# Routed experts on TensorE: one table load per four pairs, down product two pairs behind, inner transposes in two banks

## What is computed

```python
x = x + gated_scan(layernorm(x))                      # (16, 512, 256)
h = layernorm(x)
top-2 of 16 experts by softmax(h @ router_w)
routed = sum over the two: prob * (silu(h @ g_e) * (h @ u_e)) @ d_e
out = x + routed + (silu(h @ sg) * (h @ su)) @ sd      # 8192 tokens, D = 256, F = 128
```

## Time and profile before

| what | before |
|---|---|
| runs | 772.11, 772.59, 775.65 us |
| span of the profiled execution | 772.7 us, 0.1 us above the median of the runs |
| first stage | to about 430 us |
| expert stage, row transposes of pair 0 to the last down product | 430 to 692 us |
| last send of a result, then gathering and output | 697 us, to 772.7 us |
| TensorE busy, share of the span | 78% |
| granted TensorE clock in the expert stage from 440 us | 1.00 |

### The profile page before, as it was taken

How to read it: one execution, slowest core, us unless ns; L and a number is a source line. 1 busy time by engine, 2 the same in 40 slices (tenths; PEclk the granted TensorE clock), 3 DMA queues, 4 the chain that set the end, 5 groups by cost and what they waited for, 6 DMA issues and landing times.

```text
span 772.7 us, 16380 instructions
## 1 busy us (share of the span) xinstructions
PE 601.8 (78%) x3710; PEld 499.9 (65%) x3741; DVE 539.9 (70%) x1660; ACT 321.6 (42%) x733; POOL 368.3 (48%) x516
## 2 busy tenths in 40 slices
PE   3689899999999999999974788988988988970000
PEld 2467777777778777778763677877877877750000
DVE  8778898888899988897866245545445444545776
ACT  4366455565555565555452233333333333330000
POOL 3214445654545644445647356556556656661000
PEclk9789999999999999999997699999999999995555
DMA  4994111110101111101114434434544444417998
GB/s 155 275 330 125 38 40 50 56 48 34 48 34 56 55 41 41 48 34 57 57 45 171 117 120 156 155 114 155 156 131 148 146 135 146 147 50 247 379 385 293
DMA packets 82806, 96.91 MB, mean 125 GB/s; under 512 B 10142, under 2 KB 74066, under 8 KB 82774
## 3 DMA queue, kind: packets, MB, share of 16 engines
q1 hardware_dynamic: 61270, 54.32, 23.3%
q0 software_dynamic: 13056, 33.84, 12.1%
q10 hardware_dynamic: 8448, 8.39, 3.1%
HBM read 52.04 MB, written 46.57 MB: 128 GB/s over the span
## 4 chain that ended last, share of the span: by engine, by line
PE 57%; issue 12%; DVE 9%; DMA 7%; ACT 3%; POOL 2%; SPq 1%; DVEq 1%; POOLq 0%; ACTq 0%
PE gd L600 14%; PE tr L398 8%; PE gu L405 5%; DMA raw_w<-expert_results 5%; PE tr L405 5%; PE gd L436 5%; PE dn L405 5%; PE gu L617 4%; PE dn L617 4%; PE cb L398 3%; PE misc L405 2%; PE misc L527 2%; DVE tokens L1293 1%; SPq L383 1%; DMA expert_rows<-row_buf,slot 1%
## 5 line engine op out<-in xcount | busy, mean ns | idle before, releaser
L1355 POOL DMA_INDIRECT expert_rows<-row_buf,slot x128 | 132.0, 1031 | 145.3 <-DVE slot L1011 107.2
L1423 POOL DMA_INDIRECT expert_results<-raw_w,row_ids x144 | 141.6, 983 | 67.9 <-issue 35.2
L600 PE MATMUL gd<-w_hi,bx 128*128 x576 | 112.0, 297 | 0.6 <-DVE bx L1235 0.6
L436 PE MATMUL gd<-wgd,xT 128*128 128x512 f32 x384 | 103.0, 405 | 4.6 <-DVE xT L936 4.6
L398 PE MATMUL tr<-ident,row_buf 128*128 128x128 f32 x416 | 64.6, 279 | 46.4 <-issue 32.9
L1235 DVE TENSOR_TENSOR bx<-tr,bx 128x512 fp32r<-128x512 f32 x72 | 49.8, 692 | 71.6 <-ACT bx L820 63.7
L398 PEld LDWEIGHTS tr<-ident,row_buf 128*128 128x128 f32 x416 | 49.1, 142 | 64.1 <-issue 57.8
L600 PEld LDWEIGHTS gd<-w_hi,bx 128*128 128x128 f32 x576 | 85.1, 192 | 3.1 <-issue 1.0
L820 ACT ACTIVATE bx<-tr 128x512 fp32r<-128x512 f32 x71 | 42.5, 599 | 101.2 <-PE tr L398 101.2
L436 PEld LDWEIGHTS gd<-wgd,xT 128*128 128x128 f32 x384 | 71.7, 196 | 18.9 <-DVE xT L936 3.1
L1254 DVE TENSOR_TENSOR raw_w<-gd,raw_w 128x256 f32<-128x256 f32 x72 | 30.6, 425 | 64.7 <-ACT raw_w L826 64.7
(11 more groups left out here) (155 smaller groups left out, 1250.0 us busy)
## 6 DMA issues: line engine op xcount, KB each, us to landing
row_buf<-expert_rows SPq DMA_DIRECT2D x144, 130.0 KB, 2.1
raw_w<-expert_results SPq DMA_DIRECT2D x32, 512.0 KB, 10.9
tokens<-in_x SPq DMA_DIRECT2D x16, 512.0 KB, 4.9
out<-tokens ACTq DMA_DIRECT2D x16, 512.0 KB, 7.1
expert_results<-raw_w,row_ids POOLq DMA_INDIRECT x144, 2.4
expert_rows<-fill_rows SPq DMA_DIRECT2D x17, 130.0 KB, 2.6
raw_w<-in_gate_w SPq DMA_DIRECT2D x16, 128.0 KB, 4.3
raw_w<-in_up_w SPq DMA_DIRECT2D x16, 128.0 KB, 4.4
```

The source lines that it names most:

```text
L436: pe.matmul(gd[j % 2][:], xT[a][:, c, j * P:(j + 1) * P], wgd[b][:, c, :], start=(a, b, c) == (0, 0, 0), stop=False)
L600: last = pe.matmul(bgu[p][:, h * 2 * F:(h + 1) * 2 * F], bx[a][:, p, (h * KC + c) * P:(h * KC + c + 1) * P], gate_up_w[b][:, bass.ds(at[h] ...
L1355: pool.indirect_dma_start(out=rows, out_offset=bass.IndirectOffsetOnAxis(ap=slot[:, q, choice, j:j + 1], axis=0), in_=row_buf[:, q, j, :], ...
L1423: pool.indirect_dma_start(out=results, out_offset=bass.IndirectOffsetOnAxis(ap=row_ids[:, at, h:h + 1], axis=0), in_=y[:, w, h, :], in_off ...
```

## The change

TensorE's order is written as `four_pairs`. One load stands at its head, of 12 registers from word 252 + 8i on (eight from word 256 on for i = 0), and serves the tiles of pairs 4i - 2 to 4i + 3. The slot of pair q is now: row transposes of pair q + 1, inner transposes of pair q - 1, gate and up of pair q, down product of pair q - 2. The down product comes one slot later than before, and so does `results_out` on DVE. The inner transposes alternate between the banks `cb` and `misc`, and wait for ACT's copy of the pair before the last one instead of the last. The loop has the same 16 turns; behind it stand one more `four_pairs` and the last two down products, which need no load of their own. There are 18 loads in place of 37. SP and POOL are unchanged.

```diff
--- before.py
+++ after.py
@@ -578,11 +578,12 @@
 
             gate_up_w = [w[:].rearrange("q e w -> q (e w)") for w in (w_hi, w_lo)]
             down_w_flat = w_down[:].rearrange("q e d -> q (e d)")
-            btr, bgu, bth, bdn = (tr[0], tr[1]), (gd[0], gd[1]), cb, (gu, dn)
-            regs = [pe.alloc_register(f"weight_reg{k}") for k in range(6)]
-
-            def rows_transposed(q, w, p, n):
-
+            btr, bgu, bth, bdn = (tr[0], tr[1]), (gd[0], gd[1]), (cb, misc), (gu, dn)
+            regs = [pe.alloc_register(f"weight_reg{k}") for k in range(12)]
+
+            def rows_transposed(q, m, n):
+
+                p, w = m % 2, m % 4
                 pe.wait_ge(rows_in[w], 2 * W * (n + 1))
                 if known(q, 2):
                     pe.wait_ge(bx_lo, q - 1)
@@ -605,9 +606,9 @@
 
             def inner_turned(q, p):
                 pe.wait_ge(binner, q + 1)
-                if known(q, 1):
-                    pe.wait_ge(bh_ready, q)
-                transposes(bth, 0, [b_inner[:, p, h * F:(h + 1) * F] for h in range(2)], bth_done)
+                if known(q, 2):
+                    pe.wait_ge(bh_ready, q - 1)
+                transposes(bth[p], 0, [b_inner[:, p, h * F:(h + 1) * F] for h in range(2)], bth_done)
 
             def down(q, p, at):
                 pe.wait_ge(bh_ready, q + 1)
@@ -623,40 +624,35 @@
                 pe.load(use, table[0:1, bass.ds(first, count)])
                 return [pe.snap(r, min_val=0, max_val=(E - 1) * D) for r in use]
 
+            def four_pairs(i, last=False):
+
+
+                behind = 4 if known(i, 1) else 0
+                at = weight_at(8 * i + 2 * P - behind, 8 + behind)
+                for m in range(4):
+                    q = 4 * i + m
+                    here = behind + 2 * m
+                    if not (last and m == 3):
+                        rows_transposed(q + 1, (m + 1) % 4, i + (m == 3))
+                    if known(q, 1):
+                        inner_turned(q - 1, (m + 1) % 2)
+                    if isinstance(q, int) and q == 0:
+                        pe.wait_ge(w_lo_ready, E // 2)
+                        pe.wait_ge(w_down_in, W * E)
+                    gate_up(q, m % 2, at[here:here + 2])
+                    if known(q, 2):
+                        down(q - 2, m % 2, at[here - 4:here - 2])
+                return at
+
             pe.wait_ge(tab_ready, 1)
-            rows_transposed(0, 0, 0, 0)
-            at = weight_at(2 * P, 4)
-            rows_transposed(1, 1, 1, 0)
-            pe.wait_ge(w_lo_ready, E // 2)
-            pe.wait_ge(w_down_in, W * E)
-            gate_up(0, 0, at[0:2])
-            rows_transposed(2, 2, 0, 0)
-            inner_turned(0, 0)
-            gate_up(1, 1, at[2:4])
-            down(0, 0, at[0:2])
-
-            def two_pairs(q, w, n, last=False):
-
-                at = weight_at(2 * q + 2 * P - 2, 6)
-                rows_transposed(q + 1, w + 1, 1, n)
-                inner_turned(q - 1, 1)
-                gate_up(q, 0, at[2:4])
-                down(q - 1, 1, at[0:2])
-                if not last:
-                    rows_transposed(q + 2, (w + 2) % 4, 0, n + (w == 2))
-                inner_turned(q, 0)
-                gate_up(q + 1, 1, at[4:6])
-                down(q, 0, at[2:4])
-
-            two_pairs(2, 2, 0)
+            rows_transposed(0, 0, 0)
+            four_pairs(0)
             with pe.Fori(1, PAIRS // 4 - 1) as i:
-                two_pairs(4 * i, 0, i)
-                two_pairs(4 * i + 2, 2, i)
-            two_pairs(PAIRS - 4, 0, PAIRS // 4 - 1)
-            two_pairs(PAIRS - 2, 2, PAIRS // 4 - 1, last=True)
-            at = weight_at(2 * P + TILES - 2, 2)
+                four_pairs(i)
+            at = four_pairs(PAIRS // 4 - 1, last=True)
             inner_turned(PAIRS - 1, 1)
-            down(PAIRS - 1, 1, at)
+            down(PAIRS - 2, 0, at[8:10])
+            down(PAIRS - 1, 1, at[10:12])
 
 
         @block.scalar
@@ -809,7 +805,7 @@
                 act.wait_ge(bth_done, q + 1)
                 if known(q, 2):
                     act.wait_ge(bdn_done, q - 1)
-                act.activation(b_innerT[:, p, :], cb[:, 0:2 * F], ACT.Copy).then_inc(bh_ready, 1)
+                act.activation(b_innerT[:, p, :], (cb, misc)[p][:, 0:2 * F], ACT.Copy).then_inc(bh_ready, 1)
 
             def pair(q, p, last=False):
 
@@ -1253,20 +1249,19 @@
                     dve.wait_ge(bth_done, q - 1)
                 dve.tensor_tensor(b_inner[:, p, :].rearrange("q (h f) -> q h f", h=2), gu_bank(p)[:, :, F:2 * F],
                                   b_silu[:, p, :].rearrange("q (h f) -> q h f", h=2), ALU.mult).then_inc(binner, 1)
-                if known(q, 1):
-                    results_out(q - 1, (w + 3) % 4, n if w else n - 1)
+                if known(q, 2):
+                    results_out(q - 2, (w + 2) % 4, n if w >= 2 else n - 1)
 
             dve.wait_ge(bx_hi, 1)
             rows_rest(0)
-            pair(0, 0, 0)
-            pair(1, 1, 0)
-            for q in range(2, 8):
+            for q in range(8):
                 pair(q, q % 4, q // 4)
             with dve.Fori(2, PAIRS // 4 - 1) as i:
                 for w in range(4):
                     pair(4 * i + w, w, i)
             for q in range(PAIRS - 4, PAIRS):
                 pair(q, q % 4, q // 4, last=q == PAIRS - 1)
+            results_out(PAIRS - 2, 2, PAIRS // 4 - 1)
             results_out(PAIRS - 1, 3, PAIRS // 4 - 1)
```

## The result

The changed kernel takes 746.09 us as the median of four runs (743.62 to 748.6), the kernel before 772.35 us as the median of its four. The ratio is 0.964 with a 95% interval of 0.961 to 0.968: 26.3 us less. The forecast was 761.0 us, within 742 to 765. The time lies in the range, but the gain is more than twice the 11.6 us that I had worked out, so the sum was wrong.

The account below looks back on a forecast made before the run. TensorE was taken to bound the expert stage, idle behind table loads; 11.8 us over 16 turns plus 0.5 behind the loop, less 0.7 at the end, made 11.6 us less: 761.0 us, range 742 to 765.

Parts of the forecast that it names:

- What bounds the stage: Expert loop: TensorE bounds it, 86% busy, its idle time all ahead of row transposes, where table loads hold up the sequencer.
- The load that goes: Mid-turn load of slot 4i + 2 disappears: slot 25 takes 3.12 us instead of 4.00, slot 26 takes 3.02 instead of 2.97.
- the price of the load that stays: Load of 12 registers behind the loop's branch: three pieces of 16 bytes, about 1.60 us, bounds 0.67 and 3.07; chance 0.40.
- The tail: End of the stage: result copies one slot later make the last sends slip by 0.7 us, bounds 0 and 3.
- pair 71's load: Behind the loop: the load ahead of pair 71's transposes goes, with its 0.50 us of idle time.
- A: Rival on the 12-register load: an aligned load is one read whatever its length, 0.67 us, total 745.2 us; chance 0.23.
- C: Rival on the 12-register load: 246 ns per register, 3.07 us, slower than before at 786.0 us; chance 0.17.
- B2: Rival on the 12-register load: two reads, widest piece at each step, 1.12 us, total 752.8 us; chance 0.12.
- D: Rival on the loop's slots: load time goes but slots don't shorten, DVE's product or POOL too late, 770.7 us; chance 0.08.

Follow-up runs that it names:

- the grid: The kernel before with 96 table loads in 24 forms added on TensorE behind its last down product, each load's last register used in a small product; 822.92 us.
- e4_down_one_behind: The changed kernel with down product and result copies one pair behind as before, load still 12 registers from word 252 + 8i; 745.52 us, ratio 0.966 to the kernel before.
- e3_once_unaligned: The changed kernel with the down product one pair behind again and its one load per turn ten registers from word 254 + 8i; 787.91 us, 1.022 of the kernel before.

## Why the prediction was right, and where it was wrong

**What bounds the stage** was right: TensorE, with its idle time behind table loads and nowhere else. No wait for a semaphore came in its place, POOL still fits into a turn, and the granted clock stayed at 1.00.

**The load that goes** was right. The slot that had held it took 3.10 us (forecast 3.12), the next one 2.95 (3.02).

**The step that failed is the price of the load that stays.** I put the 12 registers at 1.60 us, and they take 0.85. The reading behind it was "one read costs 475 ns and the instruction 50", with pieces as wide as start and length allow. It met all the rows, 525 to 534 ns and 1476 ns, and was false in every part. By the grid the six registers from word 258 are not three reads but six steps, and the two registers at 688.2 (532 ns) are two steps, not one. The four from word 256 (525 ns) are one step of 332 ns in the grid; in the program they were TensorE's first load, and the changed kernel's first load too is dearer: eight registers take 781 ns there (the minimum of its row) and 592 to 612 elsewhere, some 0.19 us more in both cases. So I had read a price of two steps, and one of one step and a first load, as the same price of a read. That the number of pieces for 12 registers, three, came out right is luck: the same reading gives three pieces of 8 bytes for six registers from word 256, where the grid shows a step of four registers and two of one. A step of 16 bytes costs some 0.26 us and not 0.48. The difference of 0.75 us, 17 times, is 12.8 us of the 14.7 by which the gain was missed.

**The rest of the miss** in the loop is 0.08 us in the slot with the load and small amounts in slots 24 to 26, together 12.90 - 12.76 = 0.14 us a turn beyond the load (12.90 is the forecast turn with the load at its measured price), 2.2 us.

**The tail** was named and sized too small: 0.7 us forecast, 15.09 - 13.76 = 1.3 measured, within the bounds of 0 and 3, and e4_down_one_behind shows that it comes from the later down product.

**Sum of the terms as measured**: 26.1 us for the turns, 0.7 for pair 71's load (its slot takes 2.95 us in place of 3.61; 0.5 forecast), less 1.3: 25.5, against 26.3 between the medians.

**The rivals.** A gave 745.2 us, next to the result, but for 0.67 us and "whatever its length", which is false: 8, 12 and 16 registers take 0.59, 0.85 and 1.11. The argument that I held against A was false too: SP's eight registers from word 0 do start at a multiple of 16 bytes and span 32, and took 534 ns. C was right about the loads of before (one price per register, 246 ns) and wrong in extending it to the new one; e3_once_unaligned is what C describes, a load over the 2.28 us at which the prediction put the loss: 2.66 us, and 1.022 of the time before. B2, two reads, gave a load of 1.12 us and fell with it. Of D nothing came: the slots kept their length.

The Trainium skill gives 200 ns per register for loads from HBM (Runtime: NRT & Kernel Launch, Instruction fetch mechanics). The unaligned loads from SBUF here come near it, at 240 to 270 ns per register; those from a start at 16 bytes, at 69 to 77 ns per register for 8 to 16 registers, don't. The Trainium skill's floor of about 600 ns for such a load (DMA: Bandwidth & Descriptors, Latency and other measured facts) is not borne out here: one register took 306 ns, four took 332.

**What was the gain, then?** The alignment. The two factors, crossed: unaligned twice 14.39 us a turn, unaligned once 14.4 to 16.0, aligned twice 12.42, aligned once 12.76. Halving the loads made the turn longer: the load behind the branch, the dearest place, then has three steps in place of two, and the aligned load in mid-turn that goes had cost nothing (its slot takes 3.11 us with it and 3.10 without). The later down product cost 1.3 us at the end, and the second bank gave 0.8 us at most.

## What to carry to other kernels

TensorE's load of registers from SBUF was paid here in steps of some 250 ns; start such a load at a multiple of 16 bytes and take a multiple of four registers, even if some are not used, and count the steps rather than the loads. Place it behind queued work and not next to a branch: here 0.59 us disappeared in mid-turn, and 0.85 us cost 0.15 there and 0.69 behind the branch. A model that meets four rows without remainder can still be false when each row differs in two ways (first or later, one step or two); before building a sum on it, name the row that would break it.

## What the runs showed of the hardware beyond that

- TensorE's first table load took some 0.19 us more than others of its form: 781 ns against 592 for eight registers, 525 against 332 for four. That being the first is the cause was not tried.
- Unaligned loads took longer inside the loop than alone (2.66 us in the loop for ten registers, 2.40 in the grid); aligned ones did not (0.85 for twelve in the loop, 0.85 and 0.89 in the grid).
- SP's loads of eight registers took 525 ns at the least before and 525 in the median in the changed kernel, less than TensorE's 590. Whether its steps are cheaper was not tried.
- In 7 of the 16 turns of e3_once_unaligned the granted clock fell to 1.2 GHz for most of the slot behind the load's idle stretch. Those stretches were 2.2 to 2.5 us long, but so were most of those in the other 9 turns (2.2 to 2.4 us), so their length alone does not decide; from 534 us on it was every second turn, and what decides was not found. The idle stretches of before (up to 1.4 us) never did that.
